# The first layer: norm, split, keys, values and the first queries as one stage; the feed-forward weights loaded during the last heads

## The reference, cut to what matters

```python
x = L0_attn_x                                    # (2, 1024, 256)
xn = _layernorm(x)                               # (x - mean) / sqrt(var + 1e-5)
x = x + _L0_attn_ref(xn, w_q, w_kv, w_dense) + _L0_ffn_ref(xn, SU, Wscale, W_up, W_gate, W_down)
# _L0_attn_ref: 16 heads of 128 columns, 4 groups of keys and values, causal
q = xn @ w_q; k, v = split(xn @ w_kv)
probs = softmax(where(causal, q k^T * 128 ** -0.5, -inf)); out = (probs v) @ w_dense
# _L0_ffn_ref: fwht is a Walsh-Hadamard transform
h = fwht(xn * SU_ug) / 64; up, gate = (h @ W.T) * (Wscale * 64)
out = fwht(silu(gate) * up * SU_dp) @ W_down.T * Wscale_dp
```

## Time and profile before

| | us |
|---|---|
| median of 3 runs | 3763.67 (3762.89 to 3767.64) |
| the profiled execution | 3760.89 |
| its span, first to last instruction | 3759.1 |
| PE busy | 3383.6 (90%) |
| DVE busy | 2424.6 (64%) |
| ACT busy | 1569.3 (42%) |
| POOL busy | 1181.3 (31%) |
| mean granted clock of PE | 0.954 of full speed |

### The profile page before, as it was taken

How to read it: one execution, slowest core, us unless ns; L and a number is a source line. 1 busy time by engine, 2 the same in 40 slices (tenths; PEclk the granted TensorE clock), 3 DMA queues, 4 the chain that set the end, 5 groups by cost and what they waited for, 6 DMA issues and landing times. The chain is left out here.

```text
span 3759.1 us, 65234 instructions
## 1 busy us (share of the span) xinstructions
PE 3383.6 (90%) x21360; PEld 2613.8 (70%) x21360; DVE 2424.6 (64%) x4499; ACT 1569.3 (42%) x2871; POOL 1181.3 (31%) x851
## 2 busy tenths in 40 slices
PE   6799999999697999999996669999769999799997
PEld 4688888888475888888883335555348887388883
DVE  3466666666424656656655778888468887488873
ACT  2355555555233444444442316666333332333332
POOL 1202020110024666666662400000014444444444
PEclk8899999999898999999998879999979999899998
DMA  3100000000101000000000502222044443144441
GB/s 111 63 3 25 3 24 3 18 10 0 35 0 45 15 18 18 16 18 18 18 8 3 199 36 82 82 82 74 12 137 117 112 114 80 44 107 116 114 98 48
DMA packets 133296, 199.97 MB, mean 53 GB/s; under 512 B 23072, under 2 KB 78240, under 8 KB 132896
## 3 DMA queue, kind: packets, MB, share of 16 engines
q1 hardware_dynamic: 127072, 190.55, 16.3%
q0 software_dynamic: 6144, 8.39, 1.4%
HBM read 162.06 MB, written 36.57 MB: 53 GB/s over the span
## 5 line engine op out<-in xcount | busy, mean ns | idle before, releaser
L1942 DVE TENSOR_REDUCE l2h_half<-l2h_s 128x1 f32<-128x512 f32 x512 | 337.5, 686 | 50.3 <-PE l2h_s L1844 49.3
L1929 ACT ACTIVATE l2h_PT<-l2h_s 128x1024 f32<-128x1024 f32 x256 | 248.3, 1022 | 164.9 <-PE l2h_s L1854 164.8
L592 DVE TENSOR_REDUCE l0h_negtop<-l0h_sc 128x1 f32<-128x128 f32 (+7 forms) x256 | 192.8, 753 | 191.7 <-PE l0h_sc L490 187.8
L614 DVE TENSOR_TENSOR l0h_PTL<-l0h_tp,l0h_PTH 128x512 fp32r<-128x512 f32 (+3 forms) x384 | 200.4, 549 | 122.9 <-ACT l0h_PTH L672 120.0
L672 ACT ACTIVATE l0h_PTH<-l0h_tp 128x512 fp32r<-128x512 f32 (+3 forms) x384 | 175.4, 496 | 219.1 <-PE l0h_tp L501 218.9
L1844 PE MATMUL l2h_s<-l2h_K,l2h_Q 128*128 128x512 f32 x512 | 219.1, 466 | 23.5 <-DMA l2h_K<-l_split 20.4
L682 ACT ACTIVATE l0h_probs<-l0h_sc,l0h_negtop 128x128 f32<-128x128 f32 (+7 forms) x256 | 190.3, 743 | 116.1 <-DVE l0h_negtop L592 115.1
L159 POOL TENSOR_TENSOR XN<-XN,n_rstd 128x512 f32<-128x512 f32 x32 | 39.9, 1268 | 593.7 <-DVE n_rstd L140 593.7
L568 POOL TENSOR_TENSOR l0h_wq_lo<-l0h_wq,l0h_wq_hi 128x256 fp32r<-128x256 f32 x16 | 11.8, 739 | 630.0 <-ACT l0h_wq_hi L656 630.0
L516 PE MATMUL l0h_cx<-l0h_PTH,l0a_VH 128*128 128x256 f32 (+1 forms) x640 | 184.3, 288 | 17.0 <-DVE l0h_PTL L614 16.9
L501 PE MATMUL l0h_tp<-ident,l0h_probs 128*128 128x128 f32 x1152 | 177.4, 276 | 20.7 <-DVE l0h_PTL L614 20.7
(11 more groups left out here) (423 smaller groups left out, 9903.8 us busy)
## 6 DMA issues: line engine op xcount, KB each, us to landing
l3p_decb<-l_decays SPq DMA_DIRECT2D x128, 256.0 KB, 4.4
l3p_w<-L_w SPq DMA_DIRECT2D x34, 512.0 KB, 3.6
l2h_Q<-l_split SPq DMA_DIRECT2D x64, 256.0 KB
l2h_K<-l_split SPq DMA_DIRECT2D x64, 256.0 KB
l3p_prow<-l_decays SPq DMA_DIRECT2D x128, 128.0 KB, 3.1
l_split<-l2q_hi SPq DMA_DIRECT2D x16, 512.0 KB, 3.9
l_split<-l2q_lo SPq DMA_DIRECT2D x16, 512.0 KB, 3.8
l3p_wgu<-L_ffn_w_gate_up SPq DMA_DIRECT2D x32, 256.0 KB, 4.8
```

The costliest lines, as they stand in the source:

```text
L592: dve.reduce_max(negtop[:, i % 4:i % 4 + 1], sc[s % 2][:, 0:(t + 1) * P], AX_X, negate=True).then_inc(top_ready, 1)
L614: dve.tensor_tensor(PTL[part], tp[n % 2][:, 0:m * P].rearrange("p (m n) -> p m n", m=m), PTH[part].bitcast(F32), ALU.subtract).then_inc(pt ...
L1929: act.activation(PT[:, b, kb, :], s2[kb % 2][:, :], ACT.Exp, scale=L2_SCALE).then_inc(exped, 1)
L1942: dve.reduce_max(half[:, b, t, z:z + 1], bank(slot_of(i))[:, :], AX_X).then_inc(s1_read, 1)
```

## The change

`start`, the first `norm_stage`, the first `split_stage` and `l0_kv` are replaced by one block, `l0_front`. x is loaded in four transfers of 512 tokens, with the weights of keys and values behind the first. The values and keys are made in the order of the token blocks: eight products for a block, as soon as its x is split, in four PSUM banks (the mean and the variance have the other four). PE's list has the variance of the last token block behind the first eight products. wq, the dense weights and the two small masks are loaded and prepared in the same block, and the first queries are its last products. Group 0's keys and values are loaded and split in this block for batch 0 alone; those of batch 1 follow at the start of the heads. The zero that POOL adds to round a block is one column, read again for each element, instead of 1024 columns.

In `l0_heads` SP issues the nine transfers of the feed-forward weights behind its last query weights. Up and gate go into XN, whose values are no longer needed then. `l0_ffn` no longer loads anything.

```diff
+def l0_layer(nc, k, a):
+    with Stage(nc, "l0r") as st:
+        raws = L0Weights(st)
+        l0_attn(nc, k, a, raws)
+        clear_semaphores(nc)
+        l0_ffn(nc, k, a, raws)
+        clear_semaphores(nc)
...
-    pool.tensor_tensor(kv.KH[:, tok], kv.KL[:, tok].bitcast(F32), kv.zero[:, :], ALU.add).then_inc(kv.k_rounded[b], 1)
+    pool.tensor_tensor(kv.KH[:, tok], kv.KL[:, tok].bitcast(F32), kv.zero[:, :].to_broadcast([P, S]), ALU.add).then_inc(kv.k_rounded[b], 1)
...
+        mean = [st.ps(f"mean{i}") for i in range(2)]
+        var = [st.ps(f"var{i}") for i in range(2)]
+        acc = [st.ps(f"acc{i}") for i in range(4)]
...
+        NM = 2 * L0_GROUPS
+        jobs = [job for j in range(NJ) for job in [("v", 4 * j + t, j) for t in range(4)] + [("k", g, j) for g in range(L0_GROUPS)]]
+        BY_ACT = [n < NM or n % 2 == 0 for n in range(len(jobs))]
...
+                sp.dma_start(k.XT[:, :, tok(0)], rows(a["xT"])[:, :, tok(0)]).then_inc(x_loaded[0], 16)
                 for c in range(DC):
                     sp.dma_start(wkv[:, c, :], rows(a["L0_attn_w_kv"])[:, c, :]).then_inc(w_loaded, 16)
...
+                for j in range(1, NJ):
+                    sp.dma_start(k.XT[:, :, tok(j)], rows(a["xT"])[:, :, tok(j)]).then_inc(x_loaded[j], 16)
...
+                sp.dma_start(kv.wq[:, :, :], rows(a["L0_attn_w_q"])[:, :, 0:P]).then_inc(kv.wq_loaded, 16)
+                sp.dma_start(kv.wd[:, :, :], a["L0_attn_w_dense"].rearrange("(h p) n -> p h n", p=P)).then_inc(kv.wd_loaded, 16)
...
-                    if n == FIRST + NB // 2:
-                        for m in range(NB):
-                            sp.wait_ge(stored[m], 16 * (FIRST // NB + (m < FIRST % NB)))
-                        for b in range(B):
-                            load_keys(sp, kd, kv, 0, b)
-                            load_values(sp, vd, kv, 0, b)
+                    if n == len(jobs) // 2 + L0_NB // 2:
+                        for m in range(L0_NB):
+                            sp.wait_ge(kv.stored[m], 16 * (n // L0_NB + (m < n % L0_NB)))
+                        load_keys(sp, kd, kv, 0, 0)
+                        load_values(sp, vd, kv, 0, 0)
...
-                pe.wait_ge(wlo_ready, DC)
-                for n, (kind, i, j) in enumerate(jobs):
-                    if n >= 8:
-                        kept(pe, n - 8)
...
+                def mean_of(j):
+                    pe.wait_ge(x_loaded[j], 16)
+                    if j >= 2:
+                        pe.wait_ge(centred, j - 1)
...
+                def keys_and_values(j):
+                    pe.wait_ge(xlo0_ready, j + 1)
+                    pe.wait_ge(xlo1_ready, j + 1)
+                    for n in range(NM * j, NM * (j + 1)):
+                        kind, i, _ = jobs[n]
+                        if n >= 4:
+                            kept(pe, n - 4)
...
+                pe.wait_ge(set_up, 1)
+                mean_of(0)
+                mean_of(1)
+                var_of(0)
+                mean_of(2)
+                var_of(1)
+                mean_of(3)
+                var_of(2)
+                pe.wait_ge(kvlo0_ready, 1)
+                pe.wait_ge(kvlo1_ready, 1)
+                keys_and_values(0)
+                var_of(3)
+                for j in range(1, NJ):
+                    keys_and_values(j)
+                pe.wait_ge(kv.wlo_ready, 1)
+                for j in range(S // BANK):
+                    kept(pe, len(jobs) - 4 + j)
+                    split_product(pe, acc[j][:, :], lambda c: kv.wq_hi[:, c, :], lambda c: kv.wq_lo[:, c, :],
+                                  lambda c: k.XH[:, c, tok(j)], lambda c: k.XL[:, c, tok(j)]).then_inc(kv.q_made, 1)
...
+                centre(0)
+                dve.wait_ge(kvhi_ready, 1)
+                dve.tensor_tensor(w_lo[:, 0, :], wkv[:, 0, :], w_hi[:, 0, :].bitcast(F32), ALU.subtract).then_inc(kvlo0_ready, 1)
+                centre(1)
+                invert(0)
+                centre(2)
+                invert(1)
+                low_x(0)
+                centre(3)
+                invert(2)
+                low_x(1)
+                low_x(2)
+                invert(3)
+                keep(1)
+                low_x(3)
+                keep(2)
+                dve.wait_ge(consts_loaded, 32)
+                dve.tensor_copy(kv.ident[:, :], k.ident[:, :])
+                dve.tensor_copy(kv.causal[:, :], k.causal[:, :])
+                keep(3)
...
+                act.wait_ge(set_up, 2)
+                square(0)
+                root(0)
+                square(1)
+                root(1)
+                square(2)
+                high_x(0)
+                root(2)
+                square(3)
+                high_x(1)
+                for n in range(NM // 2):
+                    keep(n)
+                high_x(2)
+                for n in range(NM // 2, NM):
+                    keep(n)
+                root(3)
+                act.wait_ge(kv.wq_loaded, 16)
+                act.activation(kv.wq_hi[:, :, :], kv.wq[:, :, :], ACT.Copy).then_inc(kv.whi_ready, 1)
+                for n in range(NM, 2 * NM):
+                    keep(n)
+                high_x(3)
+                for n in range(2 * NM, NJ * NM):
+                    keep(n)
+                for j in range(S // BANK):
+                    act.wait_ge(kv.q_made, j + 1)
+                    act.activation(kv.QH[:, tok(j)], acc[j][:, :], ACT.Copy, scale=L0_SCALE).then_inc(kv.qh_ready, 1)
...
+                for j in range(NJ):
+                    pool.wait_ge(rstd_ready, j + 1)
+                    for c in range(DC):
+                        op = pool.tensor_tensor(k.XN[:, c, tok(j)], k.XN[:, c, tok(j)], rstd[:, j % 2, :], ALU.mult)
+                    op.then_inc(scaled, 1)
+                    low_x(j)
+                pool.wait_ge(kv.whi_ready, 1)
+                pool.tensor_tensor(kv.wq_lo[:, :, :], kv.wq[:, :, :], kv.wq_hi[:, :, :].bitcast(F32), ALU.subtract).then_inc(kv.wlo_ready, 1)
...
+                split_keys(pool, kv, 0, 0)
+                split_values(pool, kv, 0, 0)
...
-                query_weights(0)
-                sp.dma_start(wd[:, :, :], a["L0_attn_w_dense"].rearrange("(h p) n -> p h n", p=P)).then_inc(wd_loaded, 16)
+                for m in range(L0_NB):
+                    sp.wait_ge(kv.stored[m], 16 * (2 * L0_GROUPS * NJ // L0_NB))
+                load_keys(sp, kd, kv, 0, 1)
+                load_values(sp, vd, kv, 0, 1)
...
+                for m, name in enumerate(("L0_ffn_W_upT", "L0_ffn_W_gateT")):
+                    sp.dma_start(k.XN[:, m, :].rearrange("p (c n) -> p c n", c=DC), rows(a[name])).then_inc(raw_loaded, 16)
+                sp.dma_start(raws.rawd[:, :, :], rows(a["L0_ffn_W_downT"])).then_inc(raw_loaded, 16)
+                sp.dma_start(raws.had[:, :], a["c_had"]).then_inc(raw_loaded, 16)
...
+                sp.wait_ge(raw_loaded, 16 * 9)
...
-                project(0, 0, sc[1])
-                pe.wait_ge(mask_here, 1)
...
+                for m in range(L0_NB):
+                    pool.wait_ge(kv.stored[m], 16 * (2 * L0_GROUPS * NJ // L0_NB))
...
-                split_weights(0)
+                for b in range(1, B):
+                    split_keys(pool, kv, 0, b)
+                    split_values(pool, kv, 0, b)
...
+                    if i == 1:
+                        dve.wait_ge(cleared, 1)
...
+            raw = k.XN[:, :, :].rearrange("p m (c n) -> p m c n", c=DC)
...
-                    dve.wait_ge(loaded, 16 * NL)
-                    dve.tensor_scalar(had[:, 1, :], had[:, 0, :], -1.0, None, ALU.mult).then_inc(had_ready, 1)
+                    dve.tensor_scalar(neg[:, :], had[0][:, :], -1.0, None, ALU.mult).then_inc(had_ready, 1)
...
-        start(nc, k, a)
-        for i, (attn, ffn) in enumerate(LAYERS):
+        with Stage(nc, "x0") as sx:
+            k.XH, k.XL = sx.sb("XH", [P, DC, T], F32R), sx.sb("XL", [P, DC, T], F32R)
+            l0_layer(nc, k, a)
+        for i, (attn, ffn) in enumerate(LAYERS[1:], 1):
             norm_stage(nc, k, f"n{i}", k.XT, k.XN)
             with Stage(nc, f"x{i}") as sx:
                 if i in SPLIT_LAYERS:
```

243 lines of the change are left out of this document (138 added, 105 removed).

## The result

The changed kernel takes 3702.19 us (median of 4 runs, 3701.01 to 3702.84) against 3765.65 us of the kernel before in the same comparison: a ratio of 0.9828, 95% interval 0.9811 to 0.9845. The forecast was 3697.0, faster, with a range of 3685 to 3711.

What follows compares the result with a forecast made beforehand. PE works 90% of the span, so only its idle times at barriers can be saved: 50.2 (front) + 15.6 (feed-forward load) = 65.8 off 3760.89 gives 3695.1, median-corrected 3697.9, stated as 3697; range 3685 to 3711 us.

Steps and rivals of the forecast that it cites:

- First product: Front stage: first key/value product on PE at 24.3 us, after block 0's norm and split, with nine handovers of about 0.1.
- the first rival: Front loads issued together share engines and land together; first product 3.8 us later, total 3701; chance 0.10.
- its terms behind 12.0: Front, after block 1's mean: variance, root, reciprocal, POOL's multiplication, two ACT roundings, POOL's rest of x; summed as 11.4 us.
- 32 products of 1.36 without a gap: Front: PE runs the key and value products without waiting, 43.5 us in all, 1.5 us to spare at the tightest.
- Gain of the front: Start to first scores: first scores at 74.5 instead of 124.67 us, 50.2 earlier.
- up to 2 us faster or slower: Head 0, left out of the sum: its time may shift this much with the clock when it begins.
- Feed-forward load: Feed-forward start: early transfers save DVE's 13.0 us wait, plus 2.6 us lost to the clock; together 15.6.
- PE restarts before the fall: Feed-forward start: PE resumes before the clock drops from 2.4 to 1.2 GHz, so 2.6 us count as won.
- The second rival: Clock does not stay up: front products begin at 1.2 GHz (2.7 us), restart after heads too (2.6); total 3702; chance 0.09.
- Layers behind unchanged: Layers after the first: not touched by the change; the forecast would be wrong if they lost time.
- The third rival: POOL's rounding with a one-column zero is slow; at 10 us each it costs 78.6, total 3776; chance 0.03.
- The rule of the Trainium skill: Front: DVE's two-SBUF-input rest of block 0 could wait 1.4 us for a POOL instruction, giving 3698; not in the sum.

Runs made afterwards that it cites:

- the repeated pair: The kernel before and the changed kernel, each run once more with no edit: 3766.02 us (one run) and 3701.42 us (5 runs).
- the run without it: Changed kernel with both halves of the projection weights' rest taken by POOL, none by DVE: 3703.73 us (one run).

## Why the prediction was right, point by point

The time is within the stated range, and the change saves where and by what the forecast said. But 3702.19 lies nearer the numbers of the first two rivals (3701, 3702) than 3697, so the total does not tell them apart; the rows do.

- **First product** at 24.3: 24.11, by luck. Transfers issued together did slow one another, the first rival's mechanism, but by 0.9 us for block 0 and not the 3.8 that it put; and the second mean found the clock up, which the forecast's own range had as "1.5 lower". Besides, the forecast's sum is wrong: its terms behind 12.0 add up to 10.95, not 11.4, so they say 23.85 with the handovers. DVE's half of the rest, which "does not decide", was the last.
- **32 products of 1.36 without a gap**: without a gap, yes, at products 8, 13 and 24 too; but 1.40 each. The step that failed is the reading of a pace from the earlier trace rows as a property of the instruction. It belongs to the instruction at those addresses. With them restored, the stretch from first product to first scores measured 50.22 and 50.19, against 50.2 between the forecast's points; the terms that it names (43.5, 2.0, 2.7, 0.6, 0.7 and 0.3) make 49.8.
- **Gain of the front** 50.2: 49.25. POOL's splits ended at 70.67 and 88.81 (71.5 and 88.5 forecast), and the added split in the heads cost nothing.
- **The heads**, which the sum left out ("up to 2 us faster or slower"): 2.1 shorter, from the first scores to their last addition, which more than made up for the 0.95 that the front lacked. About 1.2 of it comes behind the second split of the query weights (819.1 to PE's last instruction, 820.3 before; 820.5 with the addresses put back), so the change of addresses, which cost in the front and in the loop, helped here. The rest fits head 0's clock: 3.4 us of it at 1.2 GHz in the trace before, none in the trace after. That is luck too.
- **Feed-forward load** 13.0 and 2.6: 13.2 (64.57 less the 51.36 by which the last addition of the heads is earlier), and 2.64 in the trace after. But the second term is a mean over executions, and there it is smaller: third copies 7.8 after the restart on the mean of five traces with the late load, 6.6 on the mean of seven with the early one, so about 1.2. "PE restarts before the fall" held in six of the seven, but in four of these the clock fell all the same, 0.8 to 1.3 us after the restart.
- **The second rival** was half right, then: the clock was down for part of this restart in five of seven executions, at less cost than its 2.6. Its other half did not come: the first products of the front ran at 2.4 GHz (0.233 us for a matmul).
- **Layers behind unchanged**: their code is, their time is not, from one execution to the next. That they lost time was a sign of being wrong by the forecast's own words, and the first pair of traces shows it (6.4 us). The forecast took a single profiled execution as the base; its layers 1 to 3 were the shortest of twelve. In the timed runs most of this averages out: the medians say 63.5 won, and the end of the first layer came 64.5 earlier in the first pair of traces (1194.05 to 1129.55) and 63.8 in the repeated pair.
- **The 5.2 us between 3697.0 and 3702.19**: 0.9 was rounded off in the forecast, 2.0 is the median of before (3765.65, not 3763.67), 1.3 to 2.0 the first layer (65.8 less 64.5 or 63.8: pace and the clock at the restarts), and 0.3 to 1.0 is left for the layers behind.
- **The third rival**, a slow rounding with one column: 1.90 instead of 2.39, the other way.
- **The rule of the Trainium skill** (SBUF — State Buffer, section "Who interferes with whom"), which would have given 1.4 us more: the lock shows, and at the place that the forecast set aside. DVE's half of the rest of x took 1.33 us beside POOL's 1.27, against 0.65 alone, and released the first product. POOL's half was done 0.54 earlier, so the lock cost the first product about 0.5 (an estimate), not 1.4. At the rest of the weights DVE took 3.09 beside POOL and 1.2 where POOL was idle (two in 2.36 in the kernel before); that cost at most 0.2, as the run without it shows.

What stays open: whether the changed kernel meets the lower clock in layers 1 to 3 more often than the kernel before. Four traces of the kernel before and its shifted forms took 2559.0 to 2565.2 there, eight of the changed forms 2561.3 to 2570.6; the ranges overlap, and twelve are too few. Also not settled is the rule for the scores: their two operands are a multiple of 256 bytes apart in both kernels, yet those of 512 columns do not go at 0.227 (of the distances below 0.25 us the median is 0.233 before and 0.231 after).

## What to carry to other kernels

A duration that is read from a trace holds for its operands where they lie: when a change moves tensors, compare the spacing of equal matmuls before and after before looking for a wait, and spend some bytes of padding where a long run of products has slowed. A profile is one execution: compare the busy time of the bottleneck engine in untouched stages, with the instruction counts beside it, and what differs there is noise of the base. Transfers with room on their queue belong under the stage ahead, and a wait can cost more than itself: here, on the mean of twelve traces, another 1.2 us of a slower restart behind it.

## What the runs showed of the hardware

- The pace of 512-column products with a weight load each depends on where their two operands lie in SBUF, by the down products on the distance of the two. By the order of allocation x starts 77824 bytes below the projection weights and 32768 below the feed-forward weights in the kernel before, both multiples of 256: 0.227 us. At remainders of 64, 128, 160 and 192 modulo 256 (kernel before with pads, the changed kernel): 0.226 to 0.241, on the mean 0.2315 to 0.2335. 128 unused bytes at one place and 672 at another made this kernel 7.5 us slower.
- After the same rest of 1.7 us the same eight matmuls took 3.67 us in one execution and 6.70 in another, at a granted clock of 1.00 and of 0.55. The Trainium skill (TensorE: Matmul & The Clock Gate, "Part 1: The HAM clock gate") says that the gate's watch runs freely and does not start with the kernel; these rows fit that.
- After the same rest of 2.92 us the clock stayed up in two of seven traces, had fallen 0.45 us before the restart in one, and fell 0.8 to 1.3 us after it in four.
- DVE's subtraction of two SBUF operands of 128x512 took 1.33 us beside POOL's and 0.65 alone.
- POOL's rounding of 128x1024 with a one-column second operand takes 1.90 us, with a full one 2.39.
